# Attention and MLP of a fused vision kernel: two stage pipelines written as one, with the MLP's norm and products at other lags and in another order

## The reference

```python
q, k = elu(qk[..., :c]) + 1.0, elu(qk[..., c:]) + 1.0
z = 1.0 / (einsum('bnhd,bhd->bnh', q, kmean) + 1e-06)
out = einsum('bnhd,bhde->bnhe', rope(q), kv) * z[..., None]
ta = out + dwconv(v, lepe_w, lepe_b)
t = shortcut + ta * act_res @ outproj_w + outproj_b
t = t + dwconv(t, cpe2_w, cpe2_b)
tn2 = layernorm(t, n2_g, n2_b)
t = t + gelu(tn2 @ fc1_w + fc1_b) @ fc2_w + fc2_b      # 128 -> 512 -> 128
```

## Time and profile before

| | |
|---|---|
| median of 3 runs | 3776.42 us (3766.5 to 3781.95) |
| the profiled execution | 3766.47 us, its span 3764.7 us |
| busy: PE, DVE, ACT, POOL | 2961.8, 2484.8, 2364.5, 1088.9 us |
| chain that ended last, by engine | PE 49%, DVE 24%, issue 11%, ACT 9%, DMA 4% |
| mean granted clock of PE | 0.926 of full |

### The profile page before, as it was taken

How to read it: one execution, slowest core, us unless ns; L and a number is a source line. 1 busy time by engine, 2 the same in 40 slices (tenths; PEclk the granted TensorE clock), 3 DMA queues, 4 the chain that set the end, 5 groups by cost and what they waited for, 6 DMA issues and landing times.

```text
span 3764.7 us, 53610 instructions
## 1 busy us (share of the span) xinstructions
PE 2961.8 (79%) x17500; PEld 1601.7 (43%) x17500; DVE 2484.8 (66%) x2565; ACT 2364.5 (63%) x2677; POOL 1088.9 (29%) x612
## 2 busy tenths in 40 slices
PE   3688876969968877787995887776998788858699
PEld 2344335435534434444552433443554344344355
DVE  5687556865568645687466964768635786476771
ACT  2787535467679744446778864543868876454484
POOL 0235102632034500363103530146210352025530
PEclk9899988989989999898998999988999999988899
DMA  2001463600200147340020034743002004465101
GB/s 69 13 1 39 117 186 113 163 9 0 76 18 0 39 125 216 109 129 9 0 88 5 0 81 113 203 131 90 9 11 82 0 0 130 122 175 141 50 0 50
DMA packets 137194, 274.36 MB, mean 73 GB/s; under 512 B 17139, under 2 KB 93622, under 8 KB 137014
## 3 DMA queue, kind: packets, MB, share of 16 engines
q1 hardware_dynamic: 137014, 272.01, 26.1%
HBM read 194.07 MB, written 77.88 MB: 72 GB/s over the span
## 4 chain that ended last, share of the span: by engine, by line
PE 49%; DVE 24%; issue 11%; ACT 9%; DMA 4%; POOL 1%; SPq 1%; DVEq 1%; ACTq 0%; POOLq 0%
PE psum L1027 31%; PE psum L1267 5%; PE psum L1047 5%; DVE work L1444 4%; DVE work L1417 4%; PE psum L1075 3%; DVE region L1544 2%; DVE psum L1435 2%; DVE region L240 2%; DVE work L1429 2%; DMA work<-scratch_dwc 2%; PE psum L1225 2%; PE psum L1226 1%; DVE region L1611 1%; ACT work L971 1%
## 5 line engine op out<-in xcount | busy, mean ns | idle before, releaser
L1498 DVE SCALAR_TENSOR_TENSOR work<-region,cols,work 128x768 f32<-128x768 f32 x288 | 392.3, 1362 | 15.1 <-DVE work L1498 7.5
L696 POOL TENSOR_TENSOR region<-region 128x768 f32<-128x768 f32 x96 | 211.1, 2203 | 370.9 <-ACT region L876 365.2
L1027 PE MATMUL psum<-region,m_cen 128*128 128x384 f32 (+1 forms) x384 | 162.8, 550 | 168.5 <-DVE region L1611 62.3
L1027 PE MATMUL psum<-region,m_fc 128*128 128x384 f32 (+1 forms) x768 | 282.8, 491 | 10.8 <-ACT work L978 10.8
L1267 PE MATMUL psum<-work,m_fc 128*128 128x384 f32 x768 | 282.5, 491 | 0.0
L660 POOL TENSOR_TENSOR work<-work 128x768 f32<-128x768 f32 x48 | 113.9, 2376 | 503.4 <-ACT work L796 416.9
L1417 DVE SCALAR_TENSOR_TENSOR work<-region,cols,work 128x768 f32<-128x768 f32 x144 | 202.2, 1430 | 78.0 <-POOL work L660 61.9
L1027 PE MATMUL psum<-work,m_avg 128*128 128x384 f32 x576 | 224.2, 514 | 15.1 <-ACT work L838 7.2
L672 POOL TENSOR_TENSOR work<-work,region 128x768 f32<-128x768 f32 x96 | 174.5, 1817 | 211.6 <-DVE work L1429 211.6
L240 DVE SCALAR_TENSOR_TENSOR region<-region,cols 128x768 f32<-128x768 f32 x192 | 223.8, 1165 | 17.9 <-POOL region L696 9.9
L978 ACT ACTIVATE work<-psum,cols 128x768 f32<-128x768 f32 x192 | 173.1, 901 | 88.2 <-PE psum L1027 85.2
(11 more groups left out here) (234 smaller groups left out, 7548.7 us busy)
## 6 DMA issues: line engine op xcount, KB each, us to landing
work<-scratch_cpe SPq DMA_DIRECT2D x192, 196.0 KB, 4.1
work<-scratch_dwc SPq DMA_DIRECT2D x192, 196.0 KB, 4.1
work<-scratch_lepe SPq DMA_DIRECT2D x192, 196.0 KB, 3.9
region<-in_tab_ch SPq DMA_DIRECT2D x48, 768.0 KB, 5.2
region<-in_x SPq DMA_DIRECT2D x48, 384.0 KB, 3.3
region<-in_tab_tok SPq DMA_DIRECT2D x48, 384.0 KB, 3.1
out<-work SPq DMA_DIRECT2D x48, 384.0 KB, 2.3
scratch_cpe<-region SPq DMA_DIRECT2D x44, 392.0 KB, 4.6
```

Of the source, the lines that this page charges most:

```text
L696: g.tensor_tensor(chain_tile(conv, n, p), chain_tile(conv, n - 1, p), chain_tile(conv, n, p), ALU.add).then_inc(tap_done[n], 1)
L1027: last = pe.matmul(psum[:, bank + s, 0:HC], weights[:, :], moving(s), start=(n == 0), stop=(n == len(terms) - 1))
L1498: v.scalar_tensor_tensor(out=by_row(tile(acc + p)), in0=prow(k, b, *TAPS[n]), scalar=tap_weight(conv, TAPS[n]), in1=by_row(tile(acc + p)), ...
```

## The change

A new helper, `overlapped`, takes several lists, each with the step at which it starts, and issues in every step first the stages of the first list and then those of the second. With the attention at step 0 and the MLP at step NB = 12, the steps in which the attention's last blocks drain already hold the MLP's first stages. The wait of ACT for the whole attention goes; a wait for f2_lepe stands in the centre term of block 0, and g_variance of block 0 waits for the last residual2. In the MLP all lags but those of the convolution's terms and taps fall by one (up from 4 to 3, g_root from 3 to 2 and so on). The order within a step changes too: on PE g_variance stands between down(0) and up(2) and no longer between down(1) and up(3); on ACT g_root, `first` and `second` stand between gelu(1) and gelu(2), where it was `first` and `second` there and g_root between gelu(2) and gelu(3); on DVE g_normalise stands between the four taps and tap_7.

```diff
+def overlapped(eng, count, runs):
+    def blocks(t):
+        return [[t - start - lag for lag, _ in stages] for start, stages in runs]
...
+        for bs, (start, stages) in zip(blocks(t), runs):
+            for b, (lag, stage) in zip(bs, stages):
+                if 0 <= b < count:
+                    stage(b, b % 2)
+        t += 1
 # POOL
-                pipelined(g, NB, [(3, ta), (1, turned)])
-                pipelined(g, NB, [(0, tap) for tap in taps])
+                overlapped(g, NB, [(0, [(3, ta), (1, turned)]), (NB, [(0, tap) for tap in taps])])
 # ACT
-                pipelined(a, NB, [(0, query_exp), (1, reciprocal), (1, lepe_centre)])
-                all_done(a, i, f2_lepe, f2_ta)
-                pipelined(a, NB, [(4, gelu(0)), tap, (6, sign), (4, gelu(1)), first, second, (4, gelu(2)), (3, g_root),
-                                  (4, gelu(3)), (2, g_squares)])
+                def cpe2_centre(b, p):
+                    if is_first(b):
+                        a.wait_ge(f2_lepe, done(i, ((6 * BLK - 1) // SP - 1) // ROWS))
+                    tap[1](b, p)
+                overlapped(a, NB, [(0, [(0, query_exp), (1, reciprocal), (1, lepe_centre)]),
+                                   (NB, [(3, gelu(0)), (0, cpe2_centre), (5, sign), (3, gelu(1)), (2, g_root), first, second,
+                                         (3, gelu(2)), (3, gelu(3)), (1, g_squares)])])
 # PE
+                    if is_first(b):
+                        pe.wait_ge(f2_t2, done(i, NB - 1))
                     pe.wait_ge(g_sq, done(i, b))
-                pipelined(pe, NB, [(4, up(0)), (5, down(3)), (4, up(1)), (4, down(0)), (4, up(2)), (4, down(1)),
-                                   (3, g_variance), (4, up(3)), (4, down(2)), (2, g_centre)])
+                overlapped(pe, NB, [(0, attention),
+                                    (NB, [(3, up(0)), (4, down(3)), (3, up(1)), (3, down(0)), (2, g_variance), (3, up(2)), (3, down(1)),
+                                          (3, up(3)), (3, down(2)), (1, g_centre)])])
 # DVE
-                pipelined(v, NB, [(1, taps[0]), (1, taps[1]), (5, x3), (1, taps[2]), (1, taps[3]), (1, tap_7), (1, tap_8),
-                                  (3, g_normalise)])
+                overlapped(v, NB, [(0, attention), (NB, [(1, taps[0]), (1, taps[1]), (4, x3), (1, taps[2]), (1, taps[3]),
+                                                       (2, g_normalise), (1, tap_7), (1, tap_8)])])
```

More of the change, by code:

```diff
@@ L98, in chained, with active @@
             step(t)
+def overlapped(eng, count, runs):
+    def blocks(t):
+        return [[t - start - lag for lag, _ in stages] for start, stages in runs]
+    def active(t):
+        found = []
+        for n, bs in enumerate(blocks(t)):
+            if any(0 <= b < count for b in bs):
+                if not all(1 <= b <= count - 2 for b in bs):
+                    return None
+                found.append(n)
+        return found
+    stop = max(start + max(lag for lag, _ in stages) for start, stages in runs) + count
+    t = 0
+    while t < stop:
+        inside, pairs = active(t), 0
+        while inside and t + 2 * pairs + 1 < stop and active(t + 2 * pairs) == inside == active(t + 2 * pairs + 1):
+            pairs += 1
+        if pairs >= 2:
+            with eng.Fori(0, pairs, 1) as k:
+                for u in range(2):
+                    for n in inside:
+                        start, stages = runs[n]
+                        for lag, stage in stages:
+                            stage(2 * k + (t + u - start - lag), (t + u - start - lag) % 2)
+            t += 2 * pairs
+            continue
+        for bs, (start, stages) in zip(blocks(t), runs):
[3 more added lines that the diff above has]
+        t += 1
 def build(nc, t, out):
@@ L1239, in project @@
                     product(6, [(w_out, static(tile(2 + p)))]).then_inc(f2_out, 1)
-                pipelined(pe, NB, [(0, query), (1, denominator), (2, attend), (3, project), (2, convolve)])
+                attention = [(0, query), (1, denominator), (2, attend), (3, project), (2, convolve)]
                 def g_centre(b, p):
@@ L1593, in middle @@
                 right = side_tap("lepe", 0, 4, 2, f2_centre)
-                pipelined(v, NB, [(2, left), (2, right), (0, query_phi), (1, weigh), (3, residual2), (2, add_taps)])
+                attention = [(2, left), (2, right), (0, query_phi), (1, weigh), (3, residual2), (2, add_taps)]
                 def tap_7(b, p):
```

## The result

The changed kernel takes 3925.6 us, median of 4 runs (3923.6 to 3937.8), where the old one took 3779.2 beside it: the ratio is 1.040, with a 95% interval of 1.037 to 1.043. The forecast was 3890 of 3776, a ratio of 1.030, range 3820 to 3945. The span grew from 3764.7 to 3922.7 us, by 158.0. One execution of one later kernel (e2) fell into a slower state (4372.5 us at a granted clock of 0.73) and is left out of all times and ratios.

A forecast was written before the change was run, and what follows sets the result against it. PE was taken to bound attention and MLP, waiting on DVE in the hand-over. Order +27.4 less hand-over 10.3 us an image gave +68 over four images; clock +47, on 3766.5: 3882, stated as 3890, range 3820 to 3945.

The forecast's parts named there:

- the rival with a fall in every step: MLP: the clock falls in every step and for longer than one fall seen, 3917 to 3942 us; chance 0.18.
- The order: MLP steps: the new order makes up(3) wait 3.3 us for gelu(2), adding 27.4 us an image.
- the order costs less than walked: Rival, MLP: the order costs about what the hand-over gives, time near 3776 us; chance 0.04.
- faster: Rival, MLP: up(3) is not held and gelu(2) starts by 8 us, period 13.2, time 3713 us; chance 0.06.
- The clock: MLP: PE's clock falls after three in four of the new waits, 1.3 us a step, +47 us over four images.
- The hand-over: From the attention's last block to the MLP's first fc product: 10.3 us gained in an image.
- costed at nothing: Hand-over: the wait for residual2(11) ahead of g_variance(0), taken as met at 770.3, before the squares at 772.
- Period at least 16.5: Sign in the MLP: the period from up(0) to up(0) is 16.5 us or more.
- Wait of up(3) for the gelu: Sign on PE in the MLP: L1027 waits for ACT L978, about 3.3 us nine times an image.
- Clock of the MLP around 0.9: Sign in the MLP: the granted clock is under 1.00, around 0.9.
- No wait for DVE L1611: Sign on PE in the MLP: no wait for DVE's g_normalise.
- From the last w_out product to the first up(0) some 22 us: Sign in the hand-over: this stretch takes some 22 us, where it is 36.9 before.

The follow-up runs named there:

- e2: Changed kernel without the joining: attention and MLP one after the other as before, MLP with new lags and order; 3924.7 us, ratio 1.041 to the old kernel.
- e9: Changed kernel plus 14 small products on PE between down(1) and up(3), in the wait for gelu(2); 3867.5 us, ratio 1.027 to the old kernel.
- e3: Changed kernel, joined with short lags, but the old order within a step on all engines; 3750.5 us, ratio 0.994 to the old kernel.
- e4: Changed kernel with one move on ACT: first and second behind gelu(2), not ahead of it; 3795.4 us, ratio 1.006 to the old kernel.
- e8: e3 with POOL's adds one step later and PE's centring of block 0 behind the last projection; 3716.2 us, ratio 0.985 to the old kernel.
- e1: Old kernel with attention and MLP joined on all engines, old lags and old order kept; 3766.0 us, ratio 0.999 to the old kernel.
- e7: e3 without the joining: short lags, old order, attention and MLP one after the other; 3742.8 us, ratio 0.992 to the old kernel.
- e10: e3 with PE's new order alone, g_variance between down(0) and up(2); 3796.1 us, ratio 1.006 to the old kernel.
- e11: e3 with DVE's new order alone, g_normalise ahead of tap_7 and tap_8; 3877.4 us, ratio 1.028 to the old kernel.
- e5: Changed kernel plus 24 small products on PE between down(1) and up(3), in the wait for gelu(2); 3961.6 us, ratio 1.050 to the old kernel.

## Why the prediction was right, and where it was off
The sign, the place of the loss and its mechanism are as forecast. Of the three terms of the sum the order came out as walked, the clock's was too small, and the hand-over's too large and partly for a wrong reason. The two misses go the same way, so they add up: 3925.6 is inside the range, but it lies in the band of the rival with a fall in every step (3917 to 3942, chance 0.18) and not at my 3890.

**The order: right.** Forecast 27.4 us an image. The steps without a fall give 16.41 unrolled (forecast 16.5) and, in e9, 16.53 in the loop (16.7). The MLP grew by 44.3 us, of which the falls are 18.3 (next point): 26.0 for the order. The rows name the gelu as what ends the wait, nine steps of each image have it, and e3 and e4 take it away by order alone. One slip of the sum is small: the old kernel's loop has four steps of the twelve and not six, so two of the 13.98 should have been 13.59, 0.8 us more an image. The rival "the order costs less than walked" and the rival "faster" are out.

**The clock: right mechanism, mis-sized term.** I took 1.3 us a step, three falls in four at 1.7. The step lengths are 19.07, 16.41, 19.56, 18.22, 19.45, 18.22, 19.38, 18.22 and 19.30; less the 17.5 of e9's first step, 16.53 in the loop and 16.41 elsewhere, the excess is 18.3 us in nine steps, 2.0 a step: eight of nine fall, and every second fall lasts over up(3) and down(2) both. The fourth image has 20.37 and 18.10 at its start, so there all nine fall and the excess is 21.1. Over the four images that is 76 us where I had 47. The rival with a fall in every step had named 72 for it; it was right on this term. That idleness is the cause is shown by e9, where filling it gives a clock of 1.00 under the same order. The Trainium skill (TensorE: Matmul & The Clock Gate, "HAM oscillation") describes a loop whose waits of some 3 to 5 us make every single pass start cold. With waits of 3.15 us the trace agrees in eight steps of nine, and the 61 us that I worked out by it was nearer than my 47.

**The hand-over: mis-sized, and the joining is not what gains.** Forecast 10.3 us gained, measured 5.6. I let the joining bring the first centring 7 us forward; it came 3.6 earlier (36.4 us after the denominator before, 32.8 now), and e2, which is not joined, has the same hand-over as the changed kernel (50.7 and 51.1). POOL's adds ahead of ta were foreseen (forecast 757.3 with this execution's 2.6 us, measured 758.05). Missed was PE's order: "project(10), convolve(11) and add_taps(11) follow" is right, but I let project(11) run at once, though g_centre of block 0 stands ahead of it in PE's list. So the wait for residual2(11), costed at nothing because it would be met at 770.3, was met at 781.3 only (778.7 without this execution's 2.6 us). On PE that cost nothing further, since PE waits for tap_8 afterwards; on DVE it is the 5.02 us ahead of residual2. Missed was also that project(10) and convolve(11) come after an idle of 3.85 us and run at half clock, 2.9 us together. e8 mends PE's queue and POOL's, and its hand-over is 9.5 us shorter than e3's in the first image and 8.0 in the others.

**The sum.** 26.0 + 18.3 - 5.6 = 38.7 us in the first image. Over the four images the order is 104 us, the clock 76 and the hand-over -24: 155 of the 158.0 by which the span grew. The other 3 us lie outside of the part that was changed. The forecast was 68 for the order and the hand-over together and 47 for the clock, 115.

**The signs to look for.** Period at least 16.5: 16.4 to 19.6. Wait of up(3) for the gelu, about 3.3 us nine times an image: 3.15. Clock of the MLP around 0.9: 0.89. "No wait for DVE L1611" (g_normalise): right, there is none at g_centre in the steady steps. "From the last w_out product to the first up(0) some 22 us": it is 15.6, for the wrong reason, since the last w_out product itself is late.

## What to carry to other kernels
Moving a stage earlier on one engine moves all that shares its queue: walk one period on every engine, not only on the two that seem to meet, with durations from rows, and look for what now stands between a result and the one that waits for it. An idle stretch of 3 us in this PE loop costs more than its length; halving it to 1.5 gave back 130 us where 59 were waited. When two pipelines are joined, the late blocks of the first must stand ahead of the early blocks of the second in each queue, on every engine. Without that the joining shortened the hand-over by 2.4 us with the old lags (e1) and lengthened it by 1.7 to 3.1 with the short ones (e3 against e7); with it, it is 6.3 us shorter than without joining (e8 against e7).

## What the runs showed of the hardware
Waits of 1.5 us in each step left the clock full in e4 (0.99 over the MLP), and so did those of 1.3 to 1.5 us in e10 (1.00 from 800 to 950). Of the six waits of 2.6 us in the loop of e11 four were followed by slow groups (2.49 to 2.92 us instead of 1.55), and even its waits of 2.26 us by groups of 1.72 to 2.25. Of the waits of 3.15 us in the changed kernel eight of nine were followed by half clock. The same wait does not always bring a fall: in e2 a step of the loop with a wait of 3.15 us kept full clock and took 16.54 us (its up(3) at 937.70, 1.56 long).

The fall does not last equally long each time either. The step lengths alternate, 18.22 and about 19.4, though each step has the same work. A pass of the loop holds two steps, but it is not the place in the pass that decides: in e2 the long steps are the second of each pass in the first image and the first of each pass in the third.

A product in fp32 shows as two matmuls, 0.11 us each at 128 columns (48 in 5.36 us). I had not reckoned with two, and so the filling of e5 was too long.
